# Eight expert tiles first, then thirty-two: moving the boundary between two routing phases, weaving the router's small products, and moving two units' products between the phases

## The reference

```python
x = x + retrieval(attention(x, ...))        # layernorm, 16 heads, one key/value head; then a linear attention
x = x + ffn(moe(x, cond_64, ...))
# moe, for T = 2048 tokens, E = 8 experts, K = 2 chosen, M = 128
logits = (x @ wt.T + repeat(g @ wg.T)) / 2
scores = softmax(logits); topk_w, topk_idx = top_k(scores, 2)
y = sum over the 2 chosen: topk_w/sum * ((leaky(x@w_gate[e]) * (x@w_up[e])) @ w_down[e])
p = (leaky(x @ sw_gate) * (x @ sw_up)) @ sw_down      # shared expert, hidden width 256
y = y + p
# ffn: relu(y @ W1 + b1) @ W2 + b2, hidden width 1024
```

## Time and profile before

| | us |
|---|---|
| median of 3 runs | 501.07 |
| lowest, highest | 499.3, 503.08 |
| the profiled execution: whole | 500.4 |
| its span in the profile | 498.8 |
| PE busy in the span | 453.2 (91%) |
| DVE, ACT, POOL busy | 344.4, 259.8, 275.8 |
| mean granted clock of PE | 0.972 |

### The profile page before, as it was taken

One profiled execution on the slowest core, in us unless ns is written; L12 is line 12 of the kernel. 1 busy time (PEld: TensorE's weight loads), 2 busy tenths in 40 slices (PEclk: granted clock), 3 DMA queues, 4 the chain that ended last, 5 costly groups with the idle time before them and its releaser, 6 DMA issues.

```text
span 498.8 us, 11724 instructions
## 1 busy us (share of the span) xinstructions
PE 453.2 (91%) x4032; PEld 399.5 (80%) x4032; DVE 344.4 (69%) x868; ACT 259.8 (52%) x515; POOL 275.8 (55%) x301
## 2 busy tenths in 40 slices
PE   6786888999999999999998895799899699999996
PEld 3675877988888998888877775789798589898886
DVE  5787898888889888888754782878664535353422
ACT  4664565766656666666551232465564254444443
POOL 5779889797979797898716477000002360606000
PEclk9999899999999999999988997999899899999999
DMA  8761008256381901010112127455642220313101
GB/s 251 132 197 34 1 2 295 97 176 216 108 281 39 350 0 32 0 33 1 34 33 74 55 105 223 157 159 162 223 137 85 64 74 22 107 34 101 40 8 42
DMA packets 51663, 52.17 MB, mean 105 GB/s; under 512 B 6692, under 2 KB 49062, under 8 KB 51624
## 3 DMA queue, kind: packets, MB, share of 16 engines
q1 hardware_dynamic: 48004, 42.98, 27.5%
q0 software_dynamic: 3072, 8.39, 5.2%
q10 hardware_dynamic: 548, 0.28, 0.2%
HBM read 22.03 MB, written 29.62 MB: 104 GB/s over the span
## 4 chain that ended last, share of the span: by engine, by line
PE 50%; POOL 16%; DVE 12%; issue 10%; DMA 5%; ACT 4%; SPq 2%; POOLq 0%; DVEq 0%; ACTq 0%
PE bank L357 7%; PE bank L359 7%; PE bank L358 7%; PE bank L362 5%; PE bank L363 5%; PE bank L1846 3%; POOL slot_x L661 3%; POOL sim L641 3%; POOL pr L626 3%; POOL rn L646 2%; ACT oT_h L806 2%; DVE den L1134 2%; DVE oT_l L1120 2%; POOL wu_l L613 2%; PE bank L1604 2%
## 5 line engine op out<-in xcount | busy, mean ns | idle before, releaser
L669 POOL DMA_INDIRECT yg<-slot_y,yrow x32 | 34.1, 1065 | 115.5 <-DMA slot_y<-yb 71.2
L646 POOL TENSOR_TENSOR rn<-sc,half 128x6 f32<-128x6 f32 (+1 forms) x48 | 60.1, 1273 | 2.9 <-DVE sc L1109 1.8
L1397 DVE TENSOR_TENSOR hl<-hw,hh 128x512 fp32r<-128x512 f32 x32 | 22.1, 692 | 55.8 <-ACT hw L929 55.8
L927 ACT ACTIVATE hh<-bank,late 128x512 fp32r<-128x512 f32 x32 | 22.0, 688 | 52.1 <-PE bank L1846 42.0
L661 POOL DMA_INDIRECT slot_x<-xs,posi x32 | 31.6, 986 | 16.5 <-issue 9.1
L362 PE MATMUL bank<-wout_h,oT_h 128*128 128x256 f32 x128 | 33.8, 301 | 6.6 <-DVE oT_l L1120 6.6
L626 POOL TENSOR_TENSOR pr<-pe,rden 128x1024 f32<-128x1024 f32 x16 | 30.4, 1903 | 13.1 <-DVE rden L1137 12.2
L357 PE MATMUL bank<-wqkv_h,xnT_h 128*128 128x384 f32 x96 | 35.4, 368 | 2.0 <-DVE sim L1095 1.3
L641 POOL TENSOR_TENSOR sim<-sim,mx 128x1040 f32<-128x1040 f32 x16 | 30.9, 1931 | 10.2 <-DVE mx L1098 10.1
L609 POOL TENSOR_TENSOR biasm<-bias,mneg 128x1040 f32<-128x1040 f32 x16 | 35.7, 2231 | 0.5 <-DMA bias<-rel_scratch 0.5
L1106 DVE TENSOR_REDUCE ss<-sq 128x6 f32<-128x384 f32 (+1 forms) x48 | 25.3, 526 | 10.8 <-ACT sq L792 10.7
(11 more groups left out here) (315 smaller groups left out, 1546.0 us busy)
## 6 DMA issues: line engine op xcount, KB each, us to landing
slot_x<-zrow SPq DMA_DIRECT2D x4, 4352.0 KB, 14.4
xq<-slot_x SPq DMA_DIRECT2D x40, 128.0 KB, 2.2
slot_y<-yb SPq DMA_DIRECT2D x20, 256.0 KB, 2.3
fstage<-in_f_W SPq DMA_DIRECT2D x4, 512.0 KB, 5.4
out<-p_all SPq DMA_DIRECT2D x8, 256.0 KB, 2.2
raw_out<-in_c_Wout SPq DMA_DIRECT2D x2, 512.0 KB, 7.9
xs<-in_x SPq DMA_DIRECT2D x1, 1024.0 KB, 8.5
stage<-in_m_wgate SPq DMA_DIRECT2D x8, 128.0 KB, 2.1
```

The lines of the kernel that those rows point to most:

```text
L646: e.tensor_tensor(rn[:, lo:hi], sc[:, lo:hi], half[:, lo:hi], ALU.pow).then_inc(sems['rn'], 1)
L669: e.indirect_dma_start(out=yg[:, g % 2, r, t, :], out_offset=None, in_=ydram.ap()[:, :], in_offset=bass.IndirectOffsetOnAxis(ap=yrow[:, g ...
```

## The change

- `BATCHES` becomes tiles 0-7, 8-11, 12-15; `FULL` becomes 8, so that phase 0 is 8 slots (4 pairs) from the first eight token tiles, and phase 1 is 32 slots. The loads of phase 0 wait for 16 scatters, those of phase 1 for the other 16. The two counts are taken from batches 0 and 2 (`COUNTED`).
- Logits: those of group 0 are woven into the output products of step 16, those of group 2 into gate(0), those of group 3 into up(1): four small matmuls after a large one. Those of group 1 take the place in step 16 where group 0's stood. `x_transpose(1)` and its upper and lower parts move forward, from the end of step 15 to before the last products of that step.
- DVE makes phase 0's slot_table before `x_lower(3)` and its slot_rows before `router_logits(2)`.
- gate(4), up(4), gate(5), up(5) and their DVE and ACT work move between the two phases (`EARLY = 6`), among the remains of pairs 2 and 3 and the first transpose of phase 1. After the slots come gate(6), up(6), down(4), down(5), gate(7), up(7), down(6), half a y_transpose, down(7).
- SP stores pairs 0 and 1, then waits for phase 1's rows and loads pair 4 and 5, and goes on from there. PE reads words 1 to 4 between the phases. The splits of W1 move from pairs 4 and 6 to pairs 6 and 8.

```diff
-BATCHES = ((0, 4), (4, 8), (12, 4))
+BATCHES = ((0, 8), (8, 4), (12, 4))
-FULL = 16
+FULL = 8
+COUNTED = (0, NB - 1)
-            return bank[(2, 6, 4, 6, 4, 0, 6, 4)[n]]
+            return bank[(2, 6, 4, 6, 1, 1, 0, 4)[n]]
-            return bank[(3, 7, 5, 7, 5, 1, 7, 5)[n]]
+            return bank[(3, 7, 5, 7, 0, 2, 1, 5)[n]]
-        EARLY = 5
+        EARLY = 6
...
 # SP
-            e.wait_ge(sems['st_x'], 16 * 2 * BATCHES[-1][0])
-            for n in range(2 * XQ):
+            e.wait_ge(sems['st_x'], 16 * 2 * BATCHES[0][1])
+            for n in range(FULL):
...
-            for s in range(PAIRS2):
-                if s >= 2:
+            store_slots(0)
+            store_slots(1)
+            e.wait_ge(sems['tab'], 4)
+            rows_ahead = [slot_row(n // 2, n % 2) for n in range(FULL, FULL + 4)]
+            e.wait_ge(sems['st_xl'], 16 * 2 * (NT - BATCHES[0][1]))
+            for n in range(FULL, FULL + 4):
+                if n % 2 == 0:
+                    e.wait_ge(sems['bx_t'], due(n // 2 - XQ + 1))
+                load_tile(n // 2, n % 2, rows_ahead[n - FULL])
+            store_slots(2)
+            load_slots(FULL_PAIRS + 2)
+            store_slots(3)
+            load_slots(FULL_PAIRS + 3)
+            for s in range(FULL_PAIRS, PAIRS2):
+                if s >= FULL_PAIRS + 2:
                     store_slots(s - 2)
...
 # ACT
-            after_xn = {-1: after_first_xn, NT: lambda: x_upper(1), NT + 1: lambda: unit_weights(U - 1)}
+            after_xn = {-1: after_first_xn, NT + 1: lambda: unit_weights(U - 1)}
-            before_uT = {NT: lambda: x_upper(2), NT + 1: lambda: router_exp(1), LAST_I: lambda: unit_gate(0)}
+            before_uT = {NT - 1: lambda: x_upper(1), NT: lambda: x_upper(2), NT + 1: lambda: router_exp(1), LAST_I: lambda: unit_gate(0)}
...
+            unit_gate(4)
+            slot_h(FULL_PAIRS - 1)
+            slot_y(FULL_PAIRS - 2)
+            unit_upper(4)
+            slot_y(FULL_PAIRS - 1)
+            unit_gate(5)
+            slot_x(FULL_PAIRS)
+            unit_upper(5)
...
 # DVE
-            after_xn = {-1: after_first_xn}
+            after_xn = {-1: after_first_xn, NT: lambda: x_lower(1)}
-            before_lower = {NT: lambda: x_lower(1), NT + 1: lambda: [last_bias(), router_places(0)], LAST_I: lambda: router_marks(1)}
+            before_lower = {NT + 1: lambda: [last_bias(), router_places(0)], LAST_I: lambda: router_marks(1)}
             unit_product(0)
+            slot_table(0)
             x_lower(3)
             unit_leak(1)
             unit_lower(0)
+            slot_rows(0)
             router_logits(2)
...
+            unit_leak(4)
+            slot_hl(FULL_PAIRS - 1)
+            unit_product(4)
+            unit_lower(4)
+            unit_leak(5)
+            slot_xl(FULL_PAIRS)
+            unit_product(5)
+            unit_lower(5)
...
 # PE
+                    woven = isinstance(i, int) and i == NT
                     for c in range(HP):
-                        upper_passes(e, bank[6][:, 0:D], (wout_h[:, c, :], wout_l[:, c, :]), oT_h[:, c, :], c == 0)
+                        upper_passes(e, bank[6][:, 0:D], (wout_h[:, c, :], wout_l[:, c, :]), oT_h[:, c, :], c == 0, skip_group_check=woven)
+                        if woven and c == 1:
+                            logits_share(0)
+                        elif woven and 2 <= c < 2 + TG:
+                            logits_tile(0, c - 2)
...
+            def logits_share(g):
+                e.wait_ge(sems['x1T_l'], due(KD * (g + 1)))
+                if g == 0:
+                    e.wait_ge(sems['a_tables'], 3)
+                elif g >= 2:
+                    e.wait_ge(sems['pos'], g - 1)
+                e.matmul(logits_at(g), pair_of[:, :], cg[:, g * TG:(g + 1) * TG, :, :], start=True, stop=False, skip_group_check=True)
...
+                        if woven is not None and 1 <= 3 * k + m <= TG:
+                            logits_tile(woven, 3 * k + m - 1)
...
-            while_retrieving = {NT: lambda: logits(0), LAST_I: lambda: up(0, (1,))}
+            while_retrieving = {NT: lambda: logits(1), LAST_I: lambda: up(0, (1,))}
-            after_z = {NT + 1: lambda: [logits(1), gate(0), logits(2)]}
-            after_av = {NT: lambda: x_transpose(2)}
+            after_z = {NT + 1: lambda: gate(0, 2)}
+            after_av = {NT - 1: lambda: x_transpose(1), NT: lambda: x_transpose(2)}
...
             gate(1)
-            up(1)
-            logits(3)
+            up(1, woven=3)
...
-            gate(4)
-            up(4)
             down(2)
             down(3)
...
+                if s in (FULL_PAIRS, FULL_PAIRS + 1):
+                    e.wait_ge(sems['hw'], s + 1)
...
+            load_word(1)
+            gate(4)
+            load_word(2)
+            slot_h_transpose(FULL_PAIRS - 1)
+            slot_down_project(FULL_PAIRS - 2)
+            up(4)
+            load_word(3)
+            slot_down_project(FULL_PAIRS - 1)
+            gate(5)
+            load_word(4)
+            slot_transpose(FULL_PAIRS)
+            up(5)
...
-            gate(5)
+            gate(6)
             slot_h_transpose(PAIRS2 - 1)
             slot_down_project(PAIRS2 - 2)
-            up(5)
+            up(6)
             slot_down_project(PAIRS2 - 1)
             down(4)
-            gate(6)
-            up(6)
             down(5)
```

More of the change, by code:

```diff
@@ L892, in _ @@
             slot_x(0)
-            for s in range(PAIRS2):
-                if s + 1 < PAIRS2:
+            for s in range(FULL_PAIRS):
+                if s + 1 < FULL_PAIRS:
                     slot_x(s + 1)
@@ L1317, in _ @@
             unit_lower(3)
-            unit_leak(4)
-            unit_product(4)
-            unit_lower(4)
             def second_bias():
@@ L1354, in _ @@
                     slot_rows(1)
-                elif s == 9:
+            unit_leak(4)
[6 more added lines that the diff above has]
+            unit_lower(5)
+            for s in range(FULL_PAIRS, PAIRS2):
+                if s + 1 < PAIRS2:
+                    slot_xl(s + 1)
+                slot_hidden(s)
+                if s >= FULL_PAIRS + 1:
+                    slot_hl(s - 1)
+                if s == 9:
                     row_shift()
@@ L1503, in body @@
                     for c in range(HP):
-                        last = e.matmul(bank[6][:, 0:D], oT_l[:, c, :], wout_h[:, c, :], start=False, stop=c == HP - 1)
+                        last = e.matmul(bank[6][:, 0:D], oT_l[:, c, :], wout_h[:, c, :], start=False, stop=c == HP - 1, skip_group_check=isinstance(i, int) and i == NT)
                     last.then_inc(sems['wo_t'], 1)
@@ L1647, in ranks, with into_hidden @@
                 dst = ranks_at(b)
-                if b >= NB - 2:
-                    e.matmul(counts_at(b - NB + 2), ones[:, :], cs[b][:, :, n], start=True, stop=True, skip_group_check=True)
+                if b in COUNTED:
+                    e.matmul(counts_at(COUNTED.index(b)), ones[:, :], cs[b][:, :, n], start=True, stop=True, skip_group_check=True)
                 e.matmul(dst, strict[:, :], ohs[b][:, :, 1:n + 1], start=True, stop=False, skip_group_check=True)
                 e.matmul(dst, ones[:, :], cs[b][:, :, 0:n], start=False, stop=True, skip_group_check=True).then_inc(sems['rank_t'], 1)
-            def into_hidden(n, offset, dst, name, parts=range(KD)):
+            def into_hidden(n, offset, dst, name, parts=range(KD), woven=None):
                 g, u = divmod(n, NS)
@@ L1656, in into_hidden, with gate @@
                     w = slice(offset + k * M, offset + (k + 1) * M)
-                    last = split_passes(e, dst[:, :], (wu_h[:, u, w], wu_l[:, u, w]), x_parts(g, k), k == 0, k == KD - 1)
+                    xh, xl = x_parts(g, k)
+                    for m, (weight, x) in enumerate(((wu_h, xh), (wu_h, xl), (wu_l, xh))):
+                        last = e.matmul(dst[:, :], weight[:, u, w], x, start=k == 0 and m == 0, stop=k == KD - 1 and m == 2, skip_group_check=woven is not None)
+                        if woven is not None and 1 <= 3 * k + m <= TG:
+                            logits_tile(woven, 3 * k + m - 1)
                 if KD - 1 in parts:
                     last.then_inc(sems[name], 1)
-            def gate(n):
+            def gate(n, woven=None):
                 if n == 0:
```

101 lines of the change are left out of this document (54 added, 47 removed).

## The result

| | before | after |
|---|---|---|
| median in this comparison, us | 502.07 | 516.29 |
| ratio | | 1.0193, interval 1.0124 to 1.0262 |
| profiled execution | 500.4 | 513.6 |
| its span, mean granted clock | 498.8, 0.972 | 512.0, 0.950 |

What follows compares the result with a forecast made beforehand. PE, busy 91% of the span, was taken as the bound, with DVE bounding the stretch before down(3). The terms -4.0 + 8.0 + 0 = +4.0 us on the 501.07 median gave 505.0 us, range 499.0 to 509.0.

Steps and rivals of the forecast that it cites:

- Ahead of the slots: Stretch up to down(3)'s last product, forecast to start at 302.6 instead of 300.81.
- the pipeline's end: End of the pipeline ahead of the slots: 1.7 us later than before, range 0 to 3.5.
- a half clock in step 16: Half clock from 252.6 to 256.0 in the pipeline's step 16 was taken to go: -1.7 us.
- a smaller batch 1: Batch 1 has four tiles instead of eight, which shortens the chain behind gate(0): -1.0 us.
- the clock in gate(0): Longer idle time ahead of gate(0) may leave it at half clock: 1.2 us taken, between 0 and 1.7.
- The second half: Up(1) to down(3): PE loses 3.4 us, but with DVE as bound the last product comes only 1.7 + 0.1 later.
- The start of phase 0: First slots: the wait for rows goes, gate_up(0) 2.9 us earlier and gate_up(3) 4.0 us earlier than before.
- Between the phases and on to the last pair: Moved products, word loads, a transpose and a wait add 8.0 us on PE between the phases.
- a rival (0.12): Loads of phase 1 come late, behind two stores on SP: costs 1 to 3.5 us, 507; chance 0.12.
- the rival for faster: Moved products not added, and the wait in mid-slots, some 2.3 us, goes with its slow clock: 496 or less; chance 0.08.
- After the slots: PE has 2.8 us less work, but it was cover for store, gather and mix: gain 0.
- The rival for the half clock: Step 16's 1.7 us loss stays and another 1.7 comes at the slots' start: 508.4; chance 0.22.

Runs made afterwards that it cites:

- e6: The changed kernel, unchanged, run again on another chip: ratio 1.0207 to the kernel before on the same chip.
- e10: The kernel before with only the batches changed to 8, 4 and 4 tiles, with what they need; phase 0 stays at 16 slots: ratio 1.0065.
- e4: The changed kernel with ten spare 512-column products, values thrown away, in PE's wait ahead of up(1): ratio 1.0159 to the kernel before.
- e9: The kernel before with only the boundary changed: phase 0 has 8 slots instead of 16, batches stay 4, 8 and 4 tiles: ratio 1.0105.
- e8: The changed kernel with spare 512-column products, values thrown away, in five of PE's waits: ratio 1.0140 to the kernel before.
- e5: The kernel before, unchanged, run again on another chip: ratio 0.9987.
- e1: The changed kernel with no logits woven into other products, all else as changed: ratio 1.0158 to the kernel before.
- e7: The kernel before with only batches (8, 4, 4 tiles) and boundary (phase 0 of 8 slots) changed, nothing woven: ratio 1.0169.
- e11: The changed kernel with gate(4) and up(4) back before the slots, gate(5) to up(7) after them: ratio 1.0242 to the kernel before.
- e17: The changed kernel with three pauses in POOL's scatters, each until ACT has made a given result: ratio 1.0172 to the kernel before.
- e2: The kernel before with only logits(2) woven into gate(0) and logits(3) into up(1): ratio 0.9980.

## Why the prediction was wrong, point by point

- *Ahead of the slots, forecast +1.8, measured +10.1.* This is the step that failed. Its first half: the pipeline's end, +1.7 forecast, +5.6 measured. The sum took off 1.7 us for a half clock in step 16 that stayed. It took off 1.0 for a smaller batch 1, and from logits(2)'s end to x_transpose(3) it is 7.9 us before and after. And it allowed 1.2 for the clock in gate(0), which lost 2.5. These three are 4.0 us, about what is missing. The first of them would not have come out in full in any case. In e6 the clock did hold through step 16, but PE then waited 2.34 us at ranks(0) for DVE's routing of eight tiles and came there only 0.7 us earlier (263.16 against 263.89). The half clock fell behind it instead (0.57 from 263 to 266.6), and gate(0) was no earlier (271.00 against 270.81). With eight tiles in the first batch gate(0) starts 4.7 to 4.9 us later, with or without weaving (after, e10); the sum had 2.6. The waits themselves came near to what was forecast: 0.88 us at ranks(0), 1.96 ahead of gate(0), 2.67 ahead of up(1).
- *The second half: "DVE is the bound in this stretch and has the same work", 3.3 us to be won back between up(1) and down(3).* Nothing was: +9.1 became +10.1. DVE was not the bound all along, because it now waited 4.05 us for logits(3), which PE made inside the slow up(1). In the kernel before, x_lower(3) to logits(3) in DVE's hands took 3.7 us; after, 7.7. That the slow clock alone did this is not shown: e4 had up(1) at full clock, and another standstill of DVE behind it (5.1 us).
- *The start of phase 0, forecast 5.8 us shorter, measured 4.9.* Right: no wait for xq, gate_up(0) 3.1 us behind down(3), gate_up(2) still waiting 2.14 for bxT_l, gate_up(3) 4.0 behind it.
- *Between the phases and on to the last pair, forecast +8.0, measured +6.8.* The size held in part by luck: it is 9.1 between the phases less 2.3 in the middle of the slots. The products cost their time, hw 0.93 (forecast 0.8). But "the second phase's loads cost nothing beside them, 1.5 us in hand" was wrong: pair 4 waited 1.78. The wait was a rival (0.12), but neither the scatters (the last issued at 314.69) nor the table (row numbers at 323.30) were late: ACT had pair 1's result for the store at 327.7, SP issued the first load 3.1 us behind that, at 330.80, 6.3 behind gate_up(3) where the sum had 4.1, and it took 4.2 to serve PE. Without the store in front (e9) it is the table that comes last. The 2.3 us came back where the wait for xq fell from 2.33 to 1.69 and the clock stayed up (1.00 from 355 to 365 against 0.83); the sum had left that to the rival for faster.
- *After the slots, forecast 0, measured +1.2.* The chain of store, gather and mix was the bound, and gate(6) and up(6) were cover only, as said. The waits were longer by 2.5 us (1.98 and 2.02 for yg instead of 1.5, 2.27 for hl as before), close to the 2.8 forecast. Behind them PE was at half clock for some 10 us instead of 3.4, which the sum had not priced; e8 filled them, and its tail was 3.0 us shorter than that of e6.
- *The rival for the half clock* gave 508.4 with 1.7 us for each stretch. The stretches were there, with the size wrong: 10 us long, 5 us each on PE. That size was no property of the kernel either: the kernel before has 13.7 us of it in another execution. I had read one trace's 3.4 us as the price. How much of the 5 us reaches the end is not shown: e8 gave back 3.4 us for three stretches, inside the intervals.
- *The range.* It held no case in which two terms fail together; the delay ahead of the slots had 0 to 3.5 us.

## What to carry to other kernels

A smaller first phase does not only start earlier: everything that the second phase needs (its table, its row numbers, its loads) falls due earlier too, so look up what is issued ahead today across the boundary that is moved. Where small work serves as cover for an engine's wait, price the wait without it before moving it, and do not book a recovery further on unless the engine named as the bound keeps its inputs on time. The length of a half-clock stretch in one trace is one execution's, and a second trace of the same kernel is the cheapest check of it.

## What the runs showed of the hardware

- During a run of indirect scatters (one in 1.26 us) on the three chips of the experiments, ACT or DVE stood still for 5 to 16 us with no releaser in the profile, in the kernel before as in the changed one. The standstills of 9 us and more ended between 1.9 us before the end of the last scatter of the run (e10) and 3.1 us behind it (e8), shorter ones also in the middle of it (e4). The first two traces have the same scatters and no such standstill; the cause is open. The kernel before is about 10 us slower on those chips (510.8 to 514.3 against 502).
- Small matmuls (16 and 8 columns) between large ones at full clock (e4): 0.03 us for the first behind a 512-column product, 0.11 for the next, and 0.32 instead of 0.23 for the 512-column product behind them.
- In one stretch the same kernel ran 3.4 us (first trace) and 13.7 us (e5) at half clock from the same product, gate(0).
- Some profiled executions (e1, e7, e9, e11, e17) reach the first output product at 54.9 to 55.3 us instead of 50.9 to 51.7, and e2 at 53.1: their first product of 384 columns, at 12.3 to 12.7 us, takes 0.69 us instead of 0.44, though the granted clock reads 1.00 in both, and some 3.4 us at half clock follow from 19.0 to 19.5. In e1, e9 and e17 that execution is the slowest of its kernel, in e7 the second slowest, in e11 the third; that it is one execution's and not the kernel's is likely, not shown. Distances were therefore compared from places behind that start, or by ratios.
